# Decoder of four layers: the last cross attention normalised before its turn, with its outputs kept feature by feature

## The reference, cut to what matters

```python
q = einsum('nkm,hmd->nhkd', query, Wq) + bq
k = einsum('nkm,hmd->nhkd', key, Wk) + bk
v = einsum('nkm,hmd->nhkd', value, Wv) + bv
scores = where(mask, -1e9, einsum('nhkd,nhjd->nhkj', q, k) / sqrt(64))
y = einsum('nhkj,nhjd->nhkd', softmax(scores), v)
concat = y.transpose(0, 2, 1, 3).reshape(4, 256, 16 * 64)
return concat @ Wo + bo
```

## Time and profile before

| what | value |
|---|---|
| median of 3 runs | 1831.85 us (1829.83 to 1833.67) |
| profiled execution, its own time | 1836.56 us |
| its span | 1834.8 us |
| busy in the span: PE, DVE, ACT, POOL | 1357.5, 1112.6, 717.4, 387.5 us |
| granted TensorE clock, mean | 0.858 of full |

### The profile page before, as it was taken

The page is one execution under the profiler, slowest core; times in us unless marked ns, Lnnn a source line. Parts: engine busy times, 40 slices in busy tenths (PEclk is TensorE's granted clock), DMA queues, the critical chain, the costliest instruction groups (busy, mean ns, idle before and its releaser), DMA issues. The chain is left out here.

```text
span 1834.8 us, 24991 instructions
## 1 busy us (share of the span) xinstructions
PE 1357.5 (74%) x8869; PEld 1036.1 (56%) x8869; DVE 1112.6 (61%) x2407; ACT 717.4 (39%) x1539; POOL 387.5 (21%) x400
## 2 busy tenths in 40 slices
PE   4888888888866897684674984757855868868785
PEld 3666666666745565561452973645643765644662
DVE  4898999999545576315556536434356738426634
ACT  4456656656313465232231212003213425645451
POOL 2565566666210100210100311000001010000000
PEclk8999998999878799796786986858977988989897
DMA  6011011010010100340001520000020002000100
GB/s 232 25 41 37 28 43 37 28 43 16 1 59 1 35 1 1 111 150 0 1 14 58 174 73 0 1 1 1 1 90 0 1 1 44 2 1 13 33 1 12
DMA packets 30554, 64.73 MB, mean 35 GB/s; under 512 B 5536, under 2 KB 16928, under 8 KB 29920
## 3 DMA queue, kind: packets, MB, share of 16 engines
q1 hardware_dynamic: 29408, 60.91, 10.5%
q0 software_dynamic: 1024, 2.23, 0.5%
HBM read 54.94 MB, written 4.13 MB: 32 GB/s over the span
## 5 line engine op out<-in xcount | busy, mean ns | idle before, releaser
L188 POOL TENSOR_TENSOR rstd<-spread,minus_half 128x4 f32<-128x4 f32 x36 | 36.9, 1024 | 988.5 <-DVE spread L170 988.5
L922 PE MATMUL l0h_scores<-l0h_k_rot,l0h_q_slots 128*128 128x128 f32 (+1 forms) x1024 | 206.4, 352 | 0.0
L922 PEld LDWEIGHTS l0h_scores<-l0h_k_rot,l0h_q_slots 128*128 128x128 f32 x1024 | 172.2, 211 | 14.6
L1013 ACT ACTIVATE l0h_scores<-l0h_scores,l0h_top 128x128 f32<-128x128 f32 (+1 forms) x256 | 100.6, 393 | 81.0 <-DVE l0h_top L1091 80.6
L1138 POOL TENSOR_TENSOR l0h_k_part<-large_weights,l0h_sines 128x512 f32<-128x512 f32 x64 | 81.3, 1271 | 168.3 <-PE l0h_scores L922 119.0
L1139 POOL TENSOR_TENSOR l0h_k_rot<-large_weights,l0h_cosines 128x512 f32<-128x512 f32 x64 | 84.0, 1313 | 0.0
L1085 DVE TENSOR_TENSOR l0h_q_slots<-l0h_q_rot,l0h_chosen 128x1024 f32<-128x1024 f32 x64 | 78.4, 1225 | 6.7
L896 PE MATMUL l0h_projected<-XT,l0h_wq 128*128 128x256 f32 x256 | 70.1, 397 | 16.2 <-ACT large_weights L984 12.8
L910 PE MATMUL l0h_scores<-l0h_key_masks,l0h_query_picks 4*128 4x128 bf16 (+1 forms) x256 | 26.0, 253 | 61.0 <-DVE l0h_probs L1108 60.9
L1450 ACT ACTIVATE l0n_probs<-l0n_scores,l0n_top 128x256 f32<-128x256 f32 x128 | 53.9, 483 | 38.8 <-DVE l0n_top L1481 38.7
L1091 DVE TENSOR_REDUCE l0h_top<-l0h_scores 128x2 f32<-128x256 f32 (+1 forms) x128 | 65.0, 548 | 5.2 <-PE l0h_scores L922 5.2
(11 more groups left out here) (767 smaller groups left out, 3592.2 us busy)
## 6 DMA issues: line engine op xcount, KB each, us to landing
l1e_experts<-in_l_experts SPq DMA_DIRECT2D x16, 768.0 KB
l0e_experts<-in_l_experts SPq DMA_DIRECT2D x15, 578.0 KB
l0h_chosen<-l0h_chosen_dram SPq DMA_DIRECT2D x64, 128.0 KB, 2.9
small_weights<-in_w_l_ffn SPq DMA_DIRECT2D x1, 4016.0 KB, 12.4
l0h_pos<-l0h_pos_dram SPq DMA_DIRECT2D x56, 64.0 KB, 2.0
large_weights<-in_w_l_xattn SPq DMA_DIRECT2D x1, 2632.0 KB, 9.0
l3f_late<-l3f_values SPq DMA_DIRECT2D x2, 1040.0 KB, 7.0
l0h_wq<-in_l_wq SPq DMA_DIRECT2D x16, 128.0 KB, 2.8
```

Source lines behind the costliest of these rows:

```text
L922: mm = nc.tensor.matmul(at[:, slot], q_slots[:, s % 2, slot, part, i * P:(i + 1) * P], k_rot[:, s % 2, part, 0:KEYS[i][1]], start=False, s ...
L1013: last = nc.scalar.activation(one, one, ACT.Exp, bias=top[:, s % 2, i, slot:slot + 1], accum_out=total[:, s % 2, i, slot:slot + 1])
```

## The change

The attention of this sublayer gets a function of its own, `l3_cross_attend`, in place of the shared `attention`.

- VectorE multiplies the probabilities by the reciprocal of their sum in SBUF, ahead of the transposes. TensorE's turning waits for that (`normed`).
- The values keep no zeros, and the multiplication with `own_parity` and `v_tmp` go.
- `weigh` has the values as stationary operand and the turned probabilities as moving one, in 16 products of 64 rows by 64 columns, each in a quarter of the array: the row half `o` is the head of the pair, the column half `j` goes with the even or odd pair. The outputs have features on partitions.
- ScalarE copies the outputs to `heads_t`, a third operation a tile; `probs_t` has two buffers.
- TensorE's order is score of the next tile, turning of the last, weighing of the one before that.
- The rows of `wo` are laid out on the host in the order of the quarters, and `close_sublayer` gets `features_t`.

```diff
+    by_quadrant = g("Wo").reshape(PAIRS // 2, 2, 2, D3, P).transpose(2, 0, 1, 3, 4).reshape(H3 * D3, P)
...
-        heads_out = sb("heads_out", [P, T, H3 * D3])
+        heads_t = sb("heads_t", [P, PAIRS, N])
...
-                    k.vchain(v, nc.vector.tensor_tensor(v_tmp[:].rearrange("p h d -> p (h d)"), out, W("bv"), ALU.add))
-                    return nc.vector.tensor_tensor(values[:, b], v_tmp[:],
-                                                   bc(k.own_parity.unsqueeze(2), [P, H3, D3]), ALU.mult)
+                    return nc.vector.tensor_tensor(values[:, b].rearrange("p h d -> p (h d)"), out, W("bv"), ALU.add)
...
-            attention(k, "l3x_att", [unit(t) for t in range(T)], D3 ** -0.5, wide_out=True)
-        close_sublayer(k, "l3x_close", heads_out[:], [W("wo")[:, c * P:(c + 1) * P] for c in range(PAIRS)], PAIRS,
-                       bias=W("bo"))
+            l3_cross_attend(k, q_t, keys, values, add, heads_t)
+        close_sublayer(k, "l3x_close", None, [W("wo")[:, c * P:(c + 1) * P] for c in range(PAIRS)], PAIRS,
+                       bias=W("bo"), features_t=[heads_t[:, c, :] for c in range(PAIRS)])
+def l3_cross_attend(k, q_t, keys, values, add, heads_t):
...
+                def turn(u):
+                    pe.wait_ge(normed.sem, normed.base + u + 1)
+
+                    if u >= 1:
+                        pe.wait_ge(turned_copied.sem, turned_copied.base + u)
+                    pairs = probs[:, u % 2].rearrange("p (x j) s -> p x (j s)", j=2)
                     for x in range(PAIRS):
+                        mm = nc.tensor.transpose(turned[:, x * P:(x + 1) * P], pairs[:, x], k.ident[:])
+                    mm.then_inc(turned_ready.sem, 1)
+
+                def weigh(u):
+                    b = u // TB
+                    pe.wait_ge(turned_copied.sem, turned_copied.base + u + 1)
+
+                    if u >= 1:
+                        pe.wait_ge(out_used.sem, out_used.base + u)
+                    for m in range(PAIRS // 2):
+                        for j in range(2):
+                            x = 2 * m + j
+                            for o in range(2):
+                                rows = slice(o * SC, (o + 1) * SC)
+                                mm = nc.tensor.matmul(outs[j * D3:(j + 1) * D3, o, m], values[rows, b, 2 * x + o],
+                                                      probs_t[rows, u % 2, x * P:(x + 1) * P], start=True, stop=True,
+                                                      skip_group_check=True)
+                    mm.then_inc(out_ready.sem, 1)
+
+                score(0)
+                for u in range(T):
+                    if u + 1 < T:
+                        score(u + 1)
+                    if u >= 1:
+                        turn(u - 1)
+                    if u >= 2:
+                        weigh(u - 2)
+                turn(T - 1)
+                weigh(T - 2)
+                weigh(T - 1)
...
+                for u in range(T):
+                    act.wait_ge(shifted.sem, shifted.base + u + 1)
+                    nc.scalar.activation(probs[:, u % 2], probs[:, u % 2], ACT.Exp, scale=D3 ** -0.5).then_inc(exp_ready.sem, 1)
+                    if u >= 1:
+                        copy_turned(u - 1)
+                    if u >= 2:
+                        copy_out(u - 2)
+                copy_turned(T - 1)
+                copy_out(T - 2)
+                copy_out(T - 1)
...
+                def find_inverse(u):
+                    v.wait_ge(exp_ready.sem, exp_ready.base + u + 1)
+                    link(v, nc.vector.tensor_reduce(total[:, u % 2], probs[:, u % 2], AX.X, ALU.add))
+                    nc.vector.reciprocal(total[:, u % 2], total[:, u % 2]).then_inc(inverse_ready.sem, 1)
+                    v.wait_ge(inverse_ready.sem, inverse_ready.base + u + 1)
+                    nc.vector.tensor_tensor(probs[:, u % 2], probs[:, u % 2], bc(total[:, u % 2].unsqueeze(2), full),
+                                            ALU.mult).then_inc(normed.sem, 1)
+
+                for u in range(T):
+                    v.wait_ge(scores_ready.sem, scores_ready.base + u + 1)
+
+                    if u >= 2:
+                        v.wait_ge(turned_ready.sem, turned_ready.base + u - 1)
+                    banks = scores[:, u % 2].rearrange("p c (g s) -> p (c g) s", s=SC)
+                    link(v, nc.vector.tensor_reduce(top[:, u % 2], banks, AX.X, ALU.max))
+                    nc.vector.tensor_tensor(probs[:, u % 2], banks, bc(top[:, u % 2].unsqueeze(2), full), ALU.subtract)\
+                        .then_inc(shifted.sem, 1)
+                    if u >= 1:
+                        find_inverse(u - 1)
+                find_inverse(T - 1)
```

More of the change, by code:

```diff
@@ L2958, in l3_xattn, with _, score @@
                  activated(k, q_t[:, x, :], bias=W("bq")[:, x:x + 1])) for x in range(PAIRS)])
-            def unit(t):
-                b = t // TB
-                def score(out):
+            l3_cross_attend(k, q_t, keys, values, add, heads_t)
+        close_sublayer(k, "l3x_close", None, [W("wo")[:, c * P:(c + 1) * P] for c in range(PAIRS)], PAIRS,
+                       bias=W("bo"), features_t=[heads_t[:, c, :] for c in range(PAIRS)])
+def l3_cross_attend(k, q_t, keys, values, add, heads_t):
+    nc = k.nc
+    with ExitStack() as ctx:
+        scores = k.ps("l3x_scores", [P, 2, 2, BANK], ctx)
+        turned = k.ps("l3x_turned", [P, 2 * BANK], ctx)
+        outs = k.ps("l3x_outs", [P, 2, PAIRS // 2, P], ctx)
+        probs = k.sb("l3x_probs", [P, 2, H3, SC], F32, ctx)
+        probs_t = k.sb("l3x_probs_t", [P, 2, 2 * BANK], F32, ctx)
+        top, total = k.sb("l3x_top", [P, 2, H3], F32, ctx), k.sb("l3x_total", [P, 2, H3], F32, ctx)
+        (scores_ready, shifted, exp_ready, inverse_ready, normed, turned_ready, turned_copied, out_ready, out_used) = k.counted(
+            "attention", "scores_ready shifted exp_ready sums_copied topped turned_ready turned_copied out_ready out_used")
+        full = [P, H3, SC]
+        with nc.Block() as block:
+            @block.tensor
+            def _(pe):
+                def score(u):
+                    b, out = u // TB, scores[:, u % 2]
+                    if u >= 2:
+                        pe.wait_ge(shifted.sem, shifted.base + u - 1)
                     for c in range(2):
-                        nc.tensor.matmul(out[:, c, :], k.ident16[:], bc(add[:, t].unsqueeze(1), [P, PAIRS, SC]),
+                        nc.tensor.matmul(out[:, c, :], k.ident16[:], bc(add[:, u].unsqueeze(1), [P, PAIRS, SC]),
                                          start=True, stop=False, skip_group_check=True)
@@ L2968, in score @@
                         mm = nc.tensor.matmul(out[:, x // 4, (x % 4) * P:(x % 4 + 1) * P],
-                                              q_t[:, x, t * P:(t + 1) * P], keys[:, x, b], start=False, stop=True,
+                                              q_t[:, x, u * P:(u + 1) * P], keys[:, x, b], start=False, stop=True,
                                               skip_group_check=True)
-                    return mm
-                def product(out, probs_t):
-                    for x in range(PAIRS):
-                        mm = nc.tensor.matmul(out[:, x * P:(x + 1) * P], probs_t[:, x * P:(x + 1) * P],
-                                              values[:, b, 2 * x:2 * x + 2, :], start=True, stop=True)
-                    return mm
@@ L2978, in unit @@
-                return (2 * BANK, H3, score, product, heads_out[:, t].rearrange("p (h d) -> p h d", h=H3))
-            attention(k, "l3x_att", [unit(t) for t in range(T)], D3 ** -0.5, wide_out=True)
-        close_sublayer(k, "l3x_close", heads_out[:], [W("wo")[:, c * P:(c + 1) * P] for c in range(PAIRS)], PAIRS,
-                       bias=W("bo"))
+                    mm.then_inc(scores_ready.sem, 1)
+                def turn(u):
[3 more added lines that the diff above has]
+                    pairs = probs[:, u % 2].rearrange("p (x j) s -> p x (j s)", j=2)
+                    for x in range(PAIRS):
+                        mm = nc.tensor.transpose(turned[:, x * P:(x + 1) * P], pairs[:, x], k.ident[:])
+                    mm.then_inc(turned_ready.sem, 1)
@@ new lines, in _, with copy_turned, copy_out @@
+                score(0)
[9 more added lines that the diff above has]
+                weigh(T - 1)
+            @block.scalar
+            def _(act):
+                def copy_turned(u):
+                    act.wait_ge(turned_ready.sem, turned_ready.base + u + 1)
+                    if u >= 2:
+                        act.wait_ge(out_ready.sem, out_ready.base + u - 1)
+                    nc.scalar.copy(probs_t[:, u % 2], turned[:]).then_inc(turned_copied.sem, 1)
+                def copy_out(u):
+                    act.wait_ge(out_ready.sem, out_ready.base + u + 1)
+                    nc.scalar.copy(heads_t[:, :, u * P:(u + 1) * P], outs[:].rearrange("p o m q -> p (o m) q"))\
+                        .then_inc(out_used.sem, 1)
```

(18 more changed lines are left out.)

3 lines of the change are left out of this document (1 added, 2 removed).

## The result

The changed kernel takes 1839.68 us in the median of 21 runs (1835.15 to 1844.37), beside 1834.11 us for the kernel before in 21 runs. The ratio is 1.0024, with a 95% interval of 1.0014 to 1.0035: slower by 2.6 to 6.4 us. Measured twice more it was 1.0020 (1.0004 to 1.0035) and 1.0020 (1.0005 to 1.0035). The forecast was no change, and the median lies above its range of 1829 to 1837. Of the 7.3 us between 1839.68 and the forecast's 1832.4, 2.3 are not the change's: the kernel before itself came out at 1834.11 in 21 runs, where three had given 1831.85. Counted from 1834.11, the difference of 5.6 us still lies above the range's +5.

The account below looks back on a forecast made before the run. VectorE was taken to bound the attention and TensorE the closing. Attention cost 7.6 us minus closing gain 7.1 us gave +0.5 us, so the median 1831.85 becomes 1832.4 us; range 1829 to 1837.

Parts of the forecast that it names:

- the tail: Attention's end, a chain with one output buffer: last maximum to end of attention grows from 9.48 to 13.24 us.
- "together 5.15", then 0.04, 1.09 and 0.03, 6.31 us.: Attention round: VectorE's five operations, hand-over to TensorE, eight transposes, hand-over back; 6.31 us against 5.19.
- "I take 16.1 and keep 14.5 as the bound.": Closing: sixty-four products without transposes take 16.1 us, 14.5 at full clock; closing falls from 23.5 to 16.4 us.
- Rival A: Attention loop: TensorE's clock falls to 1.2 GHz; total about +6.7 us, +3.6 with half the rounds; chance 0.10.
- "Sum. 7.6 - 7.1 = +0.5 us.": Whole kernel: attention costs 7.6 us, closing gains 7.1 us, net +0.5 us, or -1.1 at the bound.
- the projections at nothing: Projections: four parity-mask operations of 1.22 us go, but lie under TensorE's query products; gain 0, 4.9 us without that cover.
- the division in SBUF at 1.22: Attention loop: division reading and writing SBUF takes 1.22 us, the same as out of PSUM; nothing saved.
- weighing at 1.1: Attention loop: sixteen quarter products take 1.1 us a weighing, with bounds of 0.84 and 3.7 us.
- TensorE and ScalarE with room in the loop: Attention loop: TensorE has 4.25 us and ScalarE 3.1 us of work in a 6.31 us round, both covered.
- B: Weighing: quarters do not run together, 3.7 us a weighing; total about +8.3 us, 1840.2; chance 0.03.
- C: Attention: division gets cheap in SBUF; at 0.7 us instead of 1.22 the median would be 1828.2 us; chance 0.03.
- D: Attention loop: VectorE's new wait is not felt; six rounds at 5.1 us, total 7 us lower, 1825; chance 0.02.

Follow-up runs that it names:

- the kernel before with five copies: Five VectorE copies of X into x_in added at the head of the last sublayer of the kernel before; 337.32 us from the last product to the end.

## Why the prediction was wrong

The mechanism was right: VectorE's new wait, its place and its count, level in sum with the transposes that the closing loses. The steps that failed are sizes: the round and the tail were priced with TensorE at full clock and with hand-overs that were too short, and what follows the sublayer was put at nothing. The sum of +0.5 us is off by 2.3 us by the profiles (+2.8) and by 3 to 4 by the ratios (0.20 to 0.24%, 3.7 to 4.4 us); four terms came out larger and one smaller.

- *"together 5.15", then 0.04, 1.09 and 0.03, 6.31 us.* Measured 6.40 to 6.41. VectorE's part was right (1.26, 1.15, 1.24, 0.28, 1.22 in the round above); the hand-overs were not: 0.06 to TensorE, and 0.11 from the end of turning to VectorE, where I had used 0.03 from the chain. Six rounds: +0.6.
- *"I take 16.1 and keep 14.5 as the bound."* Measured 14.57, the bound. The clock was at full speed again when the closing began: -1.5. This was a wrong choice between two prices, and by luck it hid most of what the next point lost.
- *Rival A, the clock in the loop.* One of six rounds was cold, 7.29 in place of 6.40: +0.9. I had it as a rival with all or half the rounds, and it came as a part of the forecast's own case; the rival's 0.7 a cold round was too little, since eight transposes took 1.8 times as long and not 1.6. In the tail, where I had counted every TensorE operation at full clock, the stretch from the last maximum to the closing took 14.83 us and not 13.5: +1.3. About 1.0 of it is the fall of the clock (the last turning starts 0.91 us behind its division and takes 1.19 us, where I had 0.04 and 1.09), the rest lies in the hand-overs. I used the clock only to choose the closing's price, and it fell a few microseconds earlier. The rule that transposes don't count as busy (the Trainium skill, "TensorE: Matmul & The Clock Gate", "Part 4: PE-mode transpose") would have made this rival the forecast; the trace agrees in direction, but five rounds of six stayed warm, and no run here tells transposes from other work.
- *"Sum. 7.6 - 7.1 = +0.5 us."* With the four differences above (+0.6, -1.5, +0.9, +1.3) it is +1.7 in the sublayer, as measured (71.12 against 69.41).
- The forecast had nothing behind the sublayer, except as spread. There the changed kernel lost 1.0 to 1.3 us. The stretches show where. First the kernel before, then the changed one, then the kernel before with five copies, in two stretches each: from 38 to 62 us behind the last product (work of the last sublayer) and from 110 to 167 (the closing of its first half and the net after it):

```profile
1538.41:1562.41 24.00, 15.91 (x117) 14.99 (x116) 22.68 (x46) 8.43 (x14) 0.00 (x0) 0.79 0.39 84
1610.41:1667.41 57.00, 38.76 (x236) 28.40 (x236) 17.34 (x44) 16.25 (x25) 2.04 (x2) 0.85 0.00 1
```

```profile
1536.25:1560.25 24.00, 16.40 (x109) 15.71 (x110) 21.82 (x45) 7.57 (x13) 0.00 (x0) 0.72 0.39 84
1608.25:1665.25 57.00, 39.07 (x232) 28.88 (x232) 16.82 (x44) 15.84 (x24) 2.04 (x2) 0.82 0.00 1
```

```profile
1536.28:1560.28 24.00, 15.92 (x103) 14.75 (x102) 23.59 (x48) 8.75 (x14) 0.00 (x0) 0.72 0.39 84
1608.28:1665.28 57.00, 38.45 (x228) 27.75 (x225) 17.56 (x47) 16.78 (x26) 2.04 (x2) 0.82 0.00 1
```
In the changed kernel the same work meets a granted clock of 0.72 and 0.82 in place of 0.79 and 0.85, and the products that follow it start 170.5 us behind the last product and no longer 169.0. The unchanged program with five copies meets the same lower clocks. In the programs with three buffers whose rests were short (332.8 to 333.2 us) the two stretches read 0.79 and 0.85, in the one with 334.45 us 0.72 and 0.82. The clock's records also say what moves: in each of the profiles of the kernel before and of the changed one, the first fall of the clock behind the last product comes 74.6 us behind the first maximum, while the last product itself comes after 69.4 us in the one and 71.1 in the other. So the work moves against the clock's changes by what the sublayer gains or loses. That it is the clock that makes the rest longer is argued from these rows and was not tried by itself.

So the profiles give +1.7 and +1.1, together 2.8 us or 0.15%. This lies within all three intervals (lower ends 0.14, 0.04 and 0.05%), but the three measured values are 0.24, 0.20 and 0.20%. About 1 us, less than the intervals are wide, stays open. The differences of the three medians are 5.6, 2.7 and 1.0 us. The profiles can't close this: their executions of the changed kernel lie below the medians, and what stands ahead of the sublayer, the same code in all programs, put the first maximum anywhere from 1425.0 to 1434.5 us in the profiles of this case.

Right were: the projections at nothing (35.78 us from the mask's first operation to the first maximum, 35.80 before), the division in SBUF at 1.22, weighing at 1.1, TensorE and ScalarE with room in the loop, and the tail as a chain with the single output buffer in it. Rivals B, C and D did not happen.

## What to carry to other kernels

When an engine's new last step in a round is what another engine waits for, look at the first one's next wait on a buffer: if that is released by what it has just handed over, two buffers act as one, and a third (4 KB a partition here) turned 0.2% slower into 0.3% faster. When the terms of a sum nearly cancel, the small ones decide; the granted clock belongs in every term in which TensorE is on the path and has had gaps ahead of it, the tail above all. In a long program, an edit of a microsecond moves later stages against the changes of the clock. Here the same code behind the sublayer took 332.8 to 335.7 us by what stood ahead of it (334.4 before), and all that was seen fits the clock as the reason; so compare stretches before spans, and look at what follows an edit too.

## What the runs showed of the hardware

- Quarter products ran together when consecutive ones lay in different quarters (and banks), and mostly one by one when four in a row lay in the same one: sixteen of 64x64 by 128 columns took 1.10 us going round the quarters and 2.56 us in fours in the same one; eight whole ones took 1.95.
- From the end of the last transpose in the record to VectorE's start it was 0.11 us, from VectorE's end to TensorE's start 0.06.
- The moments of the clock's changes behind the sublayer kept their distance to the work ahead of it and not to the work behind: 74.6 us from the first maximum to the first fall behind the last product, with 69.4 or 71.1 us of sublayer in between.
- GpSimd's masks (seven small operations) took 2.68 us beside one VectorE copy of 0.7 us, 3.42 beside three and 4.47 beside six.
- At a granted clock of 1.2 GHz eight transposes took 1.97 us (1.09 at 2.4) and sixteen quarters 1.99 (1.10).
- Eight bf16 products of 512 columns in a gap of 2.9 us kept the clock up in the tail and saved 2.0 us; five ahead of every turning saved 0.9 us in the loop and lost as much in the tail, where the last turning had to wait for them.
